# Attention over a long context: denominators of two head groups summed by one stride, and maxima turned by VectorE's block transposes

## The reference

```
x  = x + xattn(layernorm(x), ctx)        # ctx: (16, 2048, 512)
q  = y @ wq + bq;  k = ctx @ wk + bk;  v = ctx @ wv + bv      # 16 heads of 32
p  = softmax(q k^T / sqrt(32))            # over the 2048 keys
out = (p v) @ wo + bo
x  = x + linear_attention_and_mlp(layernorm(x))
x  = x + fp4_ffn(layernorm(x))
```

## Time and profile before

| what | us |
|---|---|
| median of 3 runs | 3289.12 (3288.94 to 3290.74) |
| the profiled execution | 3289.7 |
| its span | 3287.9 |
| PE busy | 3192.5 (97%) |
| DVE, ACT, POOL busy | 2317.0, 1662.2, 2132.0 |

### The profile page before, as it was taken

The page is one execution under the profiler, slowest core; times in us unless marked ns, Lnnn a source line. Parts: engine busy times, 40 slices in busy tenths (PEclk is TensorE's granted clock), DMA queues, the critical chain, the costliest instruction groups (busy, mean ns, idle before and its releaser), DMA issues.

```text
span 3287.9 us, 77758 instructions
## 1 busy us (share of the span) xinstructions
PE 3192.5 (97%) x30330; PEld 2630.7 (80%) x30330; DVE 2317.0 (70%) x3915; ACT 1662.2 (51%) x2082; POOL 2132.0 (65%) x1520
## 2 busy tenths in 40 slices
PE   8999999999999999999999999948999999999999
PEld 7788888888888888888888888736888888888888
DVE  6466666666666666666666666657887688799997
ACT  3566666666666666666666666632123322321111
POOL 3388888888888888888888888754555000033332
PEclk9999999999999999999999999968999999999999
DMA  5111221212211212212222122122223332310000
GB/s 164 49 54 52 62 60 53 65 59 60 63 58 55 61 52 62 60 52 64 60 59 65 53 59 61 56 77 81 71 94 107 135 105 90 126 55 24 21 19 20
DMA packets 232248, 217.36 MB, mean 66 GB/s; under 512 B 17376, under 2 KB 181088, under 8 KB 230752
## 3 DMA queue, kind: packets, MB, share of 16 engines
q1 hardware_dynamic: 231904, 212.62, 20.8%
HBM read 174.14 MB, written 38.40 MB: 65 GB/s over the span
## 4 chain that ended last, share of the span: by engine, by line
PE 92%; DVE 4%; issue 1%; POOL 1%; ACT 1%; DMA 1%; SPq 0%; ACTq 0%; POOLq 0%; DVEq 0%
PE a_bank L103 70%; PE a_bank L1643 9%; PE a_bank L1659 6%; PE a_bank L1679 2%; PE a_bank L1669 1%; PE a_bank L854 1%; ACT x_s L1375 1%; PE a_bank L2600 1%; PE a_bank L865 1%; PE a_bank L929 0%; PE a_bank L1686 0%; POOL x_pairs L1272 0%; PE a_bank L903 0%; PE a_bank L2573 0%; DVE q_y L244 0%
## 5 line engine op out<-in xcount | busy, mean ns | idle before, releaser
L103 PE MATMUL a_bank<-x_ctx,x_wk 128*128 128x512 f32 x3072 | 794.4, 401 | 0.0
L103 PE MATMUL a_bank<-x_wv,x_ctx 128*128 128x512 f32 x3072 | 752.7, 394 | 0.0
L103 PEld LDWEIGHTS a_bank<-x_wv,x_ctx 128*128 128x128 f32 x3072 | 568.6, 188 | 118.0
L103 PEld LDWEIGHTS a_bank<-x_ctx,x_wk 128*128 128x128 f32 x3072 | 559.2, 189 | 125.1 <-issue 0.4
L1272 POOL TENSOR_TENSOR x_pairs<-x_pairs,x_s 128x1024 f32<-128x1024 f32 x256 | 613.3, 2396 | 20.1
L1518 DVE TENSOR_TENSOR x_s<-x_s,a_bank 128x1024 f32<-128x1024 f32 x512 | 609.0, 1210 | 8.1 <-ACT a_bank L1382 8.1
L1375 ACT ACTIVATE x_s<-a_bank 128x1024 f32<-128x1024 f32 x512 | 496.9, 1023 | 169.6 <-PE a_bank L1643 169.6
L1388 ACT ACTIVATE x_s<-x_s 128x2048 f32<-128x2048 f32 x256 | 488.8, 1909 | 15.3 <-DVE x_s L1518 15.2
L1269 POOL TENSOR_TENSOR x_pairs<-x_s 128x1024 f32<-128x1024 f32 x128 | 303.7, 2372 | 233.4 <-ACT x_s L1388 233.4
L1262 POOL TENSOR_TENSOR x_ctx<-x_tile_raw,x_ctx 128x512 fp32r<-128x512 f32 x248 | 320.7, 1293 | 19.4
L1643 PEld LDWEIGHTS a_bank<-x_q,x_k 32*128 32x128 f32 x8192 | 254.2, 187 | 89.3 <-issue 59.2
(11 more groups left out here) (203 smaller groups left out, 5059.1 us busy)
## 6 DMA issues: line engine op xcount, KB each, us to landing
x_tile_raw<-in_ctx SPq DMA_DIRECT2D x248, 256.0 KB, 3.7
x_staged<-shifts SPq DMA_DIRECT2D x128, 256.0 KB, 3.4
m_ff_src<-in_w_ff SPq DMA_DIRECT2D x44, 192.0 KB, 2.5
wq_ff<-m_ff_dst SPq DMA_DIRECT2D x44, 192.0 KB, 1.8
s_attT<-attT SPq DMA_DIRECT2D x16, 512.0 KB, 4.1
m_w_raw<-in_w SPq DMA_DIRECT2D x32, 256.0 KB, 2.9
f_w_in<-wq_ff SPq DMA_DIRECT2D x22, 256.0 KB, 3.3
q_x<-in_x SPq DMA_DIRECT2D x16, 256.0 KB, 4.3
```

The costliest lines, as they stand in the source:

```text
L103: mm = pe.matmul(out, lhs[a], rhs[b], start=first and n == 0, stop=last and n == 2)
```

## The change

Six things are different; the last is a reordering of the seam.

1. `fold` takes one TENSOR_TENSOR of 128x1024 per two heads in place of two of 128x512. `fold_tiles` is one maximum over four tiles, a TENSOR_REDUCE of 2048 elements per partition to 512, read from PSUM with a stride of 128 elements, in place of three TENSOR_TENSORs.
2. `fold_partitions` is new: DVE turns the 32x32 blocks of the 128x512 result into the misc bank, and one TENSOR_REDUCE over runs of 32 columns leaves 128x16. PE then turns 16 columns in one transpose (`turn_maxima`) in place of four of 128x128; it stands one product triple later than the four did. The result has the heads' rows on 16 partitions, so that the maximum over blocks, the shift and the drop are formed on 16x32 values. They are saved by SP directly, without a second transpose and without ACT's copy of the shift.
3. `add_shift` of heads 1 to 3 comes after `shift_columns`; before, two heads were ahead of the folds, one between the folds and the wait for PE, and one last.
4. The exponential is taken in four instructions of 128x1024, each after its head's shift is added. The last three of them stand after the value evacuation, the second half's drop copy and the last key evacuation as shown below.
5. `sum_up` runs in every second block on both groups: four matmuls of 256 columns. `gather_den` and the reciprocal work on two groups at once, `normalise` comes one step later.
6. At the seam, POOL adds up two more steps ahead of the next stage's first instruction, DVE's and PE's first instructions of that stage move back by one or two steps, and the first use of the output bias has its own buffer, loaded earlier; the other rows of that stage are now loaded after all denominators are done.

```diff
             def fold(s, h):
-                two = cols(h, 2)
-                late_half = bank[:, two].rearrange("p j (t s) -> p j t s", t=TPC)
-                early_half = scores_of(s)[:, two, 0:TPC]
-                dve.tensor_tensor(late_half[:, :, 0:2], late_half[:, :, 0:2], early_half[:, :, 0:2],
-                                  ALU.max).then_inc(folded, 1)
-                dve.tensor_tensor(folds[:, two], late_half[:, :, 2:4], early_half[:, :, 2:4], ALU.max).then_inc(folded, 1)
+                here = bank[:, two].rearrange("p j (t s) -> p j t s", t=TPC)
+                dve.tensor_tensor(here, here, scores_of(s)[:, two, 0:TPC], ALU.max).then_inc(folded, 1)
             def fold_tiles(s):
+                dve.wait_ge(folded, START + s.count(FOLDS, 2))
+                dve.tensor_reduce(folds[:], bank[:, 0:HG].rearrange("p j (t s) -> p j s t", t=TPC),
+                                  AX.X, ALU.max).then_inc(folded, 1)
+            def fold_partitions(s):
+                turned = bank[:, misc_bank(s)]
+                dve.wait_ge(folded, START + s.count(FOLDS, 3))
+                dve.transpose(turned, folds[:].rearrange("p j s -> p (j s)")).then_inc(folded, 1)
                 dve.wait_ge(folded, START + s.count(FOLDS, 4))
-                first, second = bank[:, 0:HG, 0:S], bank[:, 0:HG, S:2 * S]
-                dve.tensor_tensor(first, first, folds[:, :, 0], ALU.max).then_inc(folded, 1)
-                dve.tensor_tensor(folds[:, :, 1], second, folds[:, :, 1], ALU.max).then_inc(folded, 1)
-                dve.wait_ge(folded, START + s.count(FOLDS, 6))
-                dve.tensor_tensor(folds[:, :, 0], first, folds[:, :, 1], ALU.max).then_inc(folded, 1)
+                dve.tensor_reduce(part_max[:], turned.rearrange("p (c r) -> p c r", r=DH), AX.X, ALU.max
+                                  ).then_inc(folded, 1)
             def step(s):
                 if e1.exists():
                     add_shift(e1, 0)
-                    add_shift(e1, 1)
                 if s.exists():
                     fold(s, 0)
                     fold(s, 1)
                     fold_tiles(s)
-                if e1.exists():
-                    add_shift(e1, 2)
-                if s.exists():
+                    fold_partitions(s)
                     shift_columns(s)
                 if e1.exists():
-                    add_shift(e1, 3)
-                if e3.exists() and e3.half:
+                    for j in range(1, HG):
+                        add_shift(e1, j)
+                if dens and e3.half:
                     invert(e3)
...
             def sum_up(s, f):
                 pe.wait_ge(summed, START + f.count(SUMS, SUMS))
                 for j in range(HG):
-                    mm = pe.matmul(bank[rows(j), misc_bank(s), S:2 * S], ones[:], total[:, j], start=True, stop=True)
+                    mm = pe.matmul(bank[rows(j), misc_bank(s), S:3 * S].rearrange("p (g s) -> p g s", g=2), ones[:],
+                                   total[:, :, j], start=True, stop=True)
...
-                if e3.exists():
+                if e3.exists() and e3.group % 2:
                     sum_up(s, e3)
...
-                sp.wait_ge(shift_kept, START + s.count(1, 1))
-                sp.dma_start(shifts[s.n][s.k], shift_rows[cols(s.group, HG)]).then_inc(shift_saved, 16)
+                sp.wait_ge(shift_cols, START + s.count(2, 2))
+                sp.dma_start(in_rows(shifts[s.n][s.k]), maxima[:, SHIFT]).then_inc(shift_saved, 16)
...
+            late.load_first_bias(sp)
             late.load_tile(sp, FIRST)
...
-            sp.wait_ge(folds_turned, START + BLOCKS)
+            sp.wait_ge(den_done, START + BLOCKS // 2)
             late.load_output_bias(sp)
```

More of the change, by code:

```diff
@@ L574, in pool_step @@
             await_count(pool, x1_ready, s.count(plus=-1))
-            pool.tensor_tensor(xbo[s.ring(2)][:], x_t[:, s.ring(2)], rows["bo"][:], ALU.add).then_inc(xbo_ready, 1)
+            pool.tensor_tensor(xbo[s.ring(2)][:], x_t[:, s.ring(2)], rows["first_bo" if nth(s, 0) else "bo"][:], ALU.add).then_inc(xbo_ready, 1)
             rsqrt(pool, 0, s)
@@ L1273, in add_up @@
                 pool.wait_ge(summed, START + e.count(SUMS, SUMS - 1))
-                if e.back(1).exists():
-                    pool.wait_ge(den_done, START + e.count())
-                pool.tensor_tensor(total[:], pairs[:, :, 0], pairs[:, :, 1], ALU.add).then_inc(summed, 1)
+                if e.group % 2 == 0 and e.back(2).exists():
+                    pool.wait_ge(den_done, START + e.doubles())
+                pool.tensor_tensor(total[:, e.group % 2], pairs[:, :, 0], pairs[:, :, 1], ALU.add).then_inc(summed, 1)
             def ease(e):
@@ L1306, in step @@
             def step(s):
-                e1, e2, e4, past = s.back(1), s.back(2), s.back(4), s.back(PER_BATCH)
+                e1, e2, e5, past = s.back(1), s.back(2), s.back(5), s.back(PER_BATCH)
                 if e2.exists():
@@ L1311, in step @@
                     ease(e1)
-                if e4.exists() and e4.half:
-                    normalise(e4)
-                if s.at == 4 and past.exists():
+                if e5.exists() and e5.half:
+                    normalise(e5)
+                if s.at == 4 and s.exists() and past.exists():
                     finish(past)
@@ L1345, in _ @@
             end_step(BLOCKS - 1)
+            end_step(BLOCKS)
+            end_step(BLOCKS + 1)
             pool.wait_ge(scored, START + 2 * BLOCKS - 4)
             late.pool_step(pool, FIRST)
-            for k in range(4):
+            for k in range(2, 5):
                 end_step(BLOCKS + k)
@@ L1418, in step @@
                     value_item(m, 0, VALUE_BANK)
-                if s.exists():
-                    keep_shift(s)
+                if e1.exists():
+                    exp(e1, 1)
+                if s.exists() and s.half:
+                    keep_drop(s)
                 if m.exists():
@@ L1506, in shift_columns @@
+            def shift_columns(s):
+                g = s.group
+                new = NEW_MAX if s.half else g
+                dve.wait_ge(shift_moved, START + s.count(1, 1))
+                dve.tensor_reduce(maxima[:, new], bank[0:NH, misc_bank(s), 3 * S:4 * S].rearrange("p (b q) -> p q b", q=DH),
                                   AX.X, ALU.max).then_inc(shift_cols, 1)
                 dve.wait_ge(shift_cols, START + s.count(2, 1))
-                dve.tensor_reduce(columns(s)[:, :, 0], columns(s)[:, :, 2:new + 1], AX.X, ALU.max,
+                if s.back(1).exists():
+                    dve.wait_ge(shift_saved, START + s.count(16))
+                both = maxima[:, g:NEW_MAX + 1:NEW_MAX - g] if s.half else maxima[:, g:g + 1]
+                dve.tensor_reduce(maxima[:, SHIFT], both.rearrange("p k q -> p q k"), AX.X, ALU.max,
@@ L1511, in shift_columns @@
                     dve.wait_ge(shift_cols, START + s.count(2, 2))
-                    dve.tensor_reduce(columns(s)[:, :, 1], columns(s)[:, :, 0:3:2], AX.X, ALU.add).then_inc(drop_cols, 1)
+                    await_count(dve, drop_kept, s.seconds())
+                    dve.tensor_reduce(maxima[:, FALL], maxima[:, g:SHIFT + 1:SHIFT - g].rearrange("p k q -> p q k"),
+                                      AX.X, ALU.add).then_inc(drop_cols, 1)
             def add_shift(e, j):
@@ L1522, in gather @@
                 dve.wait_ge(pv_done, START + e.count(1, 1))
-                if e.back(1).exists():
-                    dve.wait_ge(den_done, START + e.count())
+                if e.back(1).exists() and e.back(1).group % 2:
+                    dve.wait_ge(den_done, START + e.back(1).doubles(1))
                 if e.half:
@@ L1597, in _ @@
             end_step(BLOCKS + 1)
+            late.add_input(dve, FIRST)
+            late.scale_input(dve, FIRST)
+            end_step(BLOCKS + 2)
+            late.normalise_input(dve, FIRST)
             late.turned_lo(dve, FIRST)
-            end_step(BLOCKS + 2)
             for n in (2, 3):
@@ L1651, in weigh @@
                 last = s.back(1)
-                pe.wait_ge(shift_kept, START + (last.count(1, 1) if last.exists() else BLOCKS))
-                if last.half:
-                    pe.wait_ge(drop_kept, START + (last.seconds(1, 1) if last.exists() else B * HG))
+                pe.wait_ge(shift_cols, START + (last.count(2, 2) if last.exists() else 2 * BLOCKS))
                 if s.from_end() == -ITEMS_AHEAD:
@@ L1776, in _ @@
             end_step(BLOCKS + 1)
+            pe.wait_ge(late.x1_ready, START + 1)
+            late.input_product(pe, SECOND)
+            end_step(BLOCKS + 2)
             late.turn_input(pe, FIRST)
-            end_step(BLOCKS + 2)
             pe.wait_ge(kept, START + HG * BLOCKS)
```

145 lines of the change are left out of this document (61 added, 84 removed).

## The result

The changed kernel takes 3375.4 us (median of four runs, 3372.1 to 3378.0), the kernel before 3289.0: ratio **1.0266**, 95% interval 1.0253 to 1.0279. The forecast was 3369, so it is slower, by the amount and in the way that was laid out. The profiled execution has a span of 3373.6 against 3287.9.

A forecast was written before the change was run, and what follows sets the result against it. PE bounds the loop at 16.16 per block; the change makes a chain over DVE and ACT set it at 16.83, +0.66. Over 121 periods +80 on 3289.7 gives 3369.7, median 3369; own range 3330 to 3430, with rivals 3300 to 3470.

The forecast's parts named there:

- A: Start of the second score product on PE, the zero point of the forecast's times within a block.
- The chain, term by term: Block's DVE folds, PE's turn, DVE additions, ACT exponentials and copies: next A at 16.67, or 16.99 in second halves.
- What the maxima had to spare ahead of PE's turn: DVE's reduction to 16 ends at 8.36, PE's transpose comes at 8.92: 0.5 to spare, less the weight load's lead.
- PE's side: PE alone in the block loop: 16.16 less 0.44 for transposes plus 0.1 for denominators gives a period of 15.8.
- The merged denominators: Denominators on PE in every second block: about 0.2 cost in blocks with them, none gained without, mean +0.1.
- What was held to be hidden: ACT's dropped copies, the table's load, POOL's sums and the reciprocals in the loop, all costed at 0.
- the load's cover in the second half: Shift table's load behind the drop's save: 0.4 of cover; if gone, up to 0.4 per second-half block.
- The seam: After the loop: POOL's 12.2 us bias wait ends, norm rows load later; taken as 0, bounds -15 and +15.
- PE's saving: Rival: ACT's string behind the turn at least 1.0 shorter, loop at PE's 15.8, 3248 us; 10%.
- The strided maximum: Rival: fold_tiles reading PSUM at stride 128 takes twice the time per element, +273, 3562 us; 10%.
- The clock: Rival: PE's new holes lower its clock, some 1.5 each, in every third block, +60, 3430 us; 12%.
- the signs named ahead: Changed profile: ACT and DVE in its chain, no idle before ACT's copies, PE idle 0.7 to 1.0 before weighted values.

The follow-up runs named there:

- v9: Changed kernel with the block transpose of the folded maxima done twice: 3448.0 us.
- v2: Changed kernel with one addition, head 1's add_shift, moved between fold_partitions and shift_columns: 3260.5 us, ratio 0.9917.
- v7: v2 with ACT's value copy also moved behind the first of the two copies of the scores: 3248.7 us, ratio 0.9877.
- v12: Kernel before the change with ACT's value copy moved behind the first copies of the scores: 3291.3 us, ratio 1.0017.
- v5: Changed kernel with the denominators summed in every block again, 128 columns each: 3381.6 us, ratio 1.0285.
- v10: v7 with the denominators summed in every block again, four products of 128 columns: 3247.3 us, ratio 0.9869.
- v8: v7 with the drop's exponential behind the last two, and the seam's first two norm rows in own buffers, loaded earlier: 3319.9 us, ratio 1.0091.
- v11: v7 with only the seam edit (first tile's norm rows in own buffers, loaded earlier, weights ahead of other rows): 3237.3 us, ratio 0.9853.
- v13: Changed kernel with the 2048-element reduction reading four neighbouring elements, so shifts are not the reference's: 3373.1 us, ratio 1.0266.

## Why the prediction was right

**The chain, term by term.** Times from A, forecast against the block shown: folds from 2.30 against 2.30; reduction of 2048, 4.67 to 6.92 against 4.70 to 6.99; block transpose 6.95 to 7.64 against 7.03 to 7.76; reduction to 16 until 8.36 against 8.48; PE's turn 8.92 against 8.74; first reduction behind it 9.06 against 9.05; the additions 9.49 to 12.96 against 9.56 to 13.02. ACT: exponential 10.74 against 10.79, key copy 11.69 against 11.76, last exponential until 14.29 against 14.31, copies 14.68 to 16.62 against 14.69 to 16.63, next A 16.67 against 16.68. The two durations that no row of before had were put at 2.25 and 0.69, and are 2.29 and 0.73. The first was worked out from rows of other sizes; the second was a choice between 0.3 and 1.4, so that it fits is partly luck. What the maxima had to spare ahead of PE's turn was put at 0.5 less the weight load's lead, and is 0.26 (v9 shows that some 0.2 of it hides work).

**The sum.** +80 was forecast, +86 measured, of which 85.6 up to the 126th A. First half: 0.51 a block forecast, 0.52 measured. Second half: 17.06 on average in the first three blocks of the four, against 16.99, and 17.16 in the last, which the working didn't have. So the mean loss is 0.71 a block and not 0.66, and 121 x 0.71 = 86. In the last of the four the third small reduction on DVE (L1527) starts 0.32 behind the second, in the two before it 0.24; why wasn't tested.

**PE's side and the order.** That PE has room for a shorter period was shown by changing the order alone: the same instructions take 3260.5 in v2. PE's side was put at 15.8, with the blocks without denominators held by ACT's copies of the first scores. v7's first half shows this: 15.82 in most blocks with denominators, where PE waits for nothing, and 15.73 in most without, held by the copies. In its second half the chain over DVE and ACT still sets the blocks (PE waits 0.2 to 0.3 for the last exponential). The mean, 15.87, is 0.31 under before, of the 0.34 forecast for PE alone. That part of the sum was right in mechanism, and v12 shows that ACT's move alone finds no such room without the change.

**The merged denominators** were put at +0.1 a block on PE's side, hidden in the changed kernel. Hidden is shown (v5). The +0.1 itself isn't: in v7's order it is +0.06 in the first half and -0.03 in the second, and without it v10 is 1.5 us faster over all, within the noise.

**What was held to be hidden.** POOL, the reciprocals (1734 ns for 256 elements) and the table's load cost nothing, as forecast: none of them stands among PE's waits in the loop. Of the load's cover in the second half, put at 0.4, v8 shows how it fails: SP's queue makes it depend on the exponential of the fall.

**The seam** was put at 0. From the 126th A to the end it is +0.5, and behind the last A -1.9: one wait of 12.2 went, one of 10.7 came. With both gone the end is 3 to 6 us shorter (v8 and v11 against v7).

**The rivals.** PE's saving (10%) did not show in this order, and does in v2's. The strided maximum (10%) falls: v13 reads contiguously in the same 2291 ns. The Trainium skill (Advanced Engine Details and Errata, PSUM Cachelines) speaks of a penalty of patterns that are not contiguous, for matmuls; for this VectorE reduction the measurement shows none, and decides. The clock (12%) falls: 1.00 in the loop, with holes of 0.8 to 1.4 us in every block. Of the signs named ahead, no idle time before ACT's copies, 0.6 of DVE behind the turn and periods of 16.7 and 17.0 were there. PE's idle time before the weighted values was 0.8 in the first half, inside the 0.7 to 1.0 named, and 1.2 to 1.3 in the second, over it. The sign in the chain of the profile can't be read: the changed kernel's chain goes back only to 2264 us, into the seam; the waits and timelines take its place.

## What to carry to other kernels

An engine at 100% tells what the time is now, not what a cheaper instruction on it is worth: write down, from one fixed event, when the other engines' chains end, and see which is next. Where a chain crosses three engines in order, what stands in each queue between its links counts as much as its own links; the same instructions in another order made 115 us of difference here, and one 0.2 us step that a save on SP waits for, moved, made some 80 (v8 against v11, 77 of them in the loop). Look for a hole (here DVE ahead of a reduction that waits for PE) and put into it what stands behind it.

## What the runs showed of the hardware

- A block transpose of 128x512 in fp32 on VectorE, from SBUF to PSUM, takes 727 ns, about as long as a reduction of 512 elements (692), and the reduction of 2048 elements 2292, contiguous or with a stride of 128 elements.
- Two exponentials of 1024 elements from SBUF in a row take 1.99 us on ACT, one of 2048 took 1.90: halving costs 0.1.
- The granted clock was 1.00 (2.4 GHz) from 200 to 2150 us in the changed kernel, with an idle time of PE before the weighted values of every block, 1.0 us on average and 1.4 at most. In the kernel before it had fallen after an idle time of 2.15: 0.64 on average from 106.2 to 110.6 us, where the lower level is 0.5 (1.2 GHz).
